# A fused four-layer graph network: the first layer's degree and weights' products behind the next block's first quarter, and two dense blocks in place of three in the third layer

## The reference

```
for each of the four layers:
    h = max(layernorm(x), 0)
    x = x + layer(h, adj)

layer 1: (adj @ h + beta * h) / (rowsum(adj) + beta) @ kernel + bias
layer 2: softmax over neighbours of adj * (h @ H_v), times h
layer 3: max([h, adj @ h] @ W.T + b, 0)
layer 4: 4-head attention over neighbours (mask adj != 0), q, k, v from h,
         out gated with x_r = h @ Ws + bs by sigmoid([out, x_r, out - x_r] @ Wb)
```

## Time and profile before

| | |
|---|---|
| median of three runs | 1193.59 us (1185.4, 1193.59, 1194.25) |
| the profiled execution's own time | 1189.68 us |
| its span | 1188.0 us |
| mean granted TensorE clock over the span | 0.85 of full speed |
| TensorE busy | 895.1 us, 75% of the span |
| VectorE busy | 822.4 us, 69% |
| ScalarE busy | 687.1 us, 58% |
| GpSimd busy | 509.9 us, 43% |
| HBM traffic | 162 GB/s over the span |

### The profile page before, as it was taken

One profiled execution on the slowest core, in us unless ns is written; L12 is line 12 of the kernel. 1 busy time (PEld: TensorE's weight loads), 2 busy tenths in 40 slices (PEclk: granted clock), 3 DMA queues, 4 the chain that ended last, 5 costly groups with the idle time before them and its releaser, 6 DMA issues.

```text
span 1188.0 us, 25534 instructions
## 1 busy us (share of the span) xinstructions
PE 895.1 (75%) x5768; PEld 569.3 (48%) x5768; DVE 822.4 (69%) x2230; ACT 687.1 (58%) x3070; POOL 509.9 (43%) x526
## 2 busy tenths in 40 slices
PE   4979999999999352666667469997667788888750
PEld 1535555556455221555556334554444555555540
DVE  7388879879788774666665761121655888888788
ACT  4999879987977031434433351000455778888762
POOL 4002767735333434555555401666214444444420
PEclk9999988988989575676665679998897999999985
DMA  9556657657450125444444538984233444444421
GB/s 367 192 207 244 241 205 290 231 203 262 170 188 27 54 86 169 133 134 134 127 121 119 179 109 343 356 290 116 89 126 111 121 116 119 120 123 122 119 72 71
DMA packets 109354, 196.19 MB, mean 165 GB/s; under 512 B 21152, under 2 KB 93088, under 8 KB 103488
## 3 DMA queue, kind: packets, MB, share of 16 engines
q1 hardware_dynamic: 84368, 74.10, 19.8%
q10 hardware_dynamic: 8448, 82.99, 18.0%
q0 software_dynamic: 16432, 37.97, 11.7%
HBM read 166.17 MB, written 25.97 MB: 162 GB/s over the span
## 4 chain that ended last, share of the span: by engine, by line
PE 42%; DVE 22%; issue 17%; ACT 7%; another core or an unknown queue 2%; DVEq 2%; SPq 1%; DMA 1%; POOL 1%; ACTq 0%; POOLq 0%
PE ps L1877 7%; PE ps L1768 7%; PE ps L1852 4%; ACT unread L936 4%; PE ps L1931 4%; DVE work L1265 4%; PE ps L1922 3%; DVE work L1575 3%; PE ps L1794 2%; PE ps L1836 2%; DVE work L1266 2%; PE ps L1720 2%; PE ps L1716 2%; PE ps L1845 1%
## 5 line engine op out<-in xcount | busy, mean ns | idle before, releaser
L936 ACT ACTIVATE unread<-work 128x128 bf16<-128x128 f32 x1024 | 300.7, 295 | 6.9 <-ACT unread L936 2.1
L1768 PE MATMUL ps<-work,h_wide 128*128 128x512 f32 x512 | 241.8, 629 | 17.3 <-ACT h_wide L848 17.3
L936 ACT ACTIVATION_READ_ACCUMULATOR unread<-work 128x1 f32 x1024 | 191.6, 187 | 0.0
L755 POOL DMA_INDIRECT work<-in_adj_rows,adj_stage x120 | 157.3, 1311 | 60.1 <-issue 32.9
L1768 PEld LDWEIGHTS ps<-work,h_wide 128*128 128x128 f32 x512 | 101.3, 203 | 140.3 <-issue 138.6
L797 POOL DMA_INDIRECT work<-h_table,stage x105 | 100.2, 954 | 126.7 <-DMA h_table<-h_wide 59.3
L797 POOL DMA_INDIRECT work<-kv_table,node_flat x93 | 89.1, 958 | 121.7 <-PE ps L1941 77.5
L1575 DVE CUSTOM_DVE_ANT_0 work<-ps,work 128x512 f32<-128x512 f32 x168 | 116.2, 747 | 22.0 <-PE ps L1922 20.0
L1931 PE MATMUL ps<-ident,work 128*128 128x128 f32 x648 | 95.9, 281 | 42.6 <-issue 22.6
L1029 ACT ACTIVATE work<-work 128x512 f32<-128x512 f32 x165 | 117.2, 713 | 11.9 <-DVE work L1584 7.8
L797 POOL DMA_INDIRECT work<-h_table,node_flat x93 | 88.5, 951 | 71.8 <-issue 38.6
(11 more groups left out here) (230 smaller groups left out, 1655.7 us busy)
## 6 DMA issues: line engine op xcount, KB each, us to landing
work<-in_adj_rows ACTq DMA_DIRECT2D x38, 2048.0 KB
work<-adj_table SPq DMA_DIRECT2D x66, 192.0 KB
work<-in_adj_rows SPq DMA_DIRECT2D x6, 2048.0 KB
mask_table<-work SPq DMA_DIRECT2D x43, 128.0 KB
work<-mask_table SPq DMA_DIRECT2D x43, 128.0 KB
work<-kv_table SPq DMA_DIRECT2D x43, 128.0 KB
adj_table<-work SPq DMA_DIRECT2D x42, 128.0 KB
work<-in_adj_rows SPq DMA_DIRECT2D x66, 64.0 KB
```

Of the source, the lines that this page charges most:

```text
L755: nc.gpsimd.indirect_dma_start(out=ag[:, h, c, :], out_offset=None, in_=adj_rows, in_offset=bass.IndirectOffsetOnAxis(ap=adj_stage[:, h // ...
L936: ins = nc.scalar.activation(unread[:, m % (MQ // 2) * TB + t, :], ring[:, q, m, t * P:(t + 1) * P], ACT.Abs, accum_out=seen[:, b, t, q * ...
L1768: ins = mm(ps[:, 0, :], h_sb[:, q * MQ + m, :], ring[:, q, m, :], start=(q + m == 0), stop=False)
```

## The change

**First layer.** TensorE's degree and weights' products of block nb, up to now at the end of that block's instructions, are a function `products(nb)`, which is called one block later: after the next block's first quarter and the positions. The positions, which stood ahead of the first quarter in the loop, stand behind it. At the end, behind the last block, they follow `places(NB - 1)`. On VectorE the copy of the block's sums to `aggT` stands between the last quarter's `half_sum` and `quarter_sum`; `place(last)` stands ahead of the first quarter's `degp`, which waits for the degree products of the block before; and `code(last, 1)` stands ahead of the second quarter's sum.

**Third layer.** DB is 2 and EACH 2, and FIXED becomes 5 by its formula: two blocks are dense, 24 tiles sparse, and a quad is followed by two dense products. ScalarE waits for all stored rows before it issues the dense loads from the third slot on, six of them in place of ten. All blocks are turned and added inside the series of quads, at two places (`quad_of_unit(T * nb + T - 1) + 2`). The list of indices is the same one; its sparse part begins four tiles earlier.

```
--- before.py
+++ after.py
@@ -56,12 +56,12 @@
 FLAT = QUADS + TURN + NBUF
 OWN_ROW = NB * P * T * TB
 ZERO_ROW = OWN_ROW + T * P
-DB = 3
+DB = 2
 DT = DB * TB
 FIXED = (T - DT) // NBUF2 - 1
 PLAIN = T // NBUF - 1
 EARLY = 4 * MQ
-EACH = (DB * T - EARLY) // (FIXED * NBUF2)
+EACH = 2
 MOST2 = (T - DT) * NP // NBUF2
 FT = 8
 GROUPS = T // FT
@@ -992,6 +992,8 @@
 
 
             act.wait_ge(slot_full[1], 16 * (NB + 1))
+            for b in range(TB):
+                act.wait_ge(row_stored[b], rows_of_before(3))
             settle(act)
             for s in range(2, DB * NQ):
                 nb, q = s // NQ, s % NQ
@@ -1001,8 +1003,8 @@
                 act.dma_start(ring2[:, q, :, :], adj_block(nb, q)).then_inc(slot_full[q], 16)
                 if nb and q == NQ - 1:
                     dense_out(nb - 1)
+            dense_out(DB - 1)
             deviations(3, slice(LAST_GROUPS[0], LAST_GROUPS[1]))
-            dense_out(DB - 1)
 
             normalise(3)
 
@@ -1258,13 +1260,18 @@
 
                 return count, tiles, firsts
 
-            def reduce_slot(nb, q):
+            def reduce_slot(nb, q, last=None):
 
                 dve.wait_ge(slot_full[q], 16 * nb + 16 if not isinstance(nb, int) else 16 * (nb + 1))
                 link = Link(dve, link_sum, 2, nb * NQ + q)
                 link(nc.vector.tensor_tensor(half_sum, ring[:, q, 0:MQ // 2, :], ring[:, q, MQ // 2:MQ, :], ALU.add))
+                if q == NQ - 1:
+                    dve.wait_ge(agg_done, nb + 1)
+                    nc.vector.tensor_copy(aggT[:, :], ps[:, 0, :]).then_inc(agg_out, 1)
                 link(nc.vector.tensor_tensor(quarter_sum, half_sum[:, 0:MQ // 4, :], half_sum[:, MQ // 4:MQ // 2, :], ALU.add))
                 link.end()
+                if last is not None:
+                    place(last)
                 if q == 0:
                     dve.wait_ge(deg_done, nb + 1)
                 nc.vector.tensor_tensor(degp[:, q, :], quarter_sum[:, 0, :], quarter_sum[:, 1, :],
@@ -1293,9 +1300,8 @@
 
             def block0(nb, last, before):
 
-                reduce_slot(nb, 0)
+                reduce_slot(nb, 0, last)
                 if last is not None:
-                    place(last)
                     code(last, 0)
                 if before is not None:
                     list_quarters(before, 3)
@@ -1304,9 +1310,10 @@
                     update(last)
                 if before is not None:
                     lists(before, 3)
+                if last is not None:
+                    code(last, 1)
                 reduce_slot(nb, 1)
                 if last is not None:
-                    code(last, 1)
                     list_quarters(last, 0)
                 reduce_slot(nb, 2)
                 if last is not None:
@@ -1314,8 +1321,6 @@
                     code(last, 2)
                     list_quarters(last, 1)
                 reduce_slot(nb, 3)
-                dve.wait_ge(agg_done, nb + 1)
-                nc.vector.tensor_copy(aggT[:, :], ps[:, 0, :]).then_inc(agg_out, 1)
                 if last is not None:
                     lists(last, 1)
                     code(last, 3)
@@ -1511,7 +1516,7 @@
                                         ALU.add).then_inc(dense_read, 1)
 
             def dense_added(j):
-                for nb in range(DB - 1):
+                for nb in range(DB):
                     if j == quad_of_unit(T * nb + T - 1) + 2:
                         add_block(nb)
                         dve.wait_ge(dense_read, nb + 1)
@@ -1532,8 +1537,7 @@
                     ins = nc.vector.bn_stats(stats[:, t, :], x_sb[:, t, :])
                 return ins
 
-            sparse_quads(dve, step2, dense_added, lambda: add_block(DB - 1))
-            dve.wait_ge(dense_read, DB)
+            sparse_quads(dve, step2, dense_added)
             products = node_terms(3)
             half = FT // 2
             rest2(2, slice(FT, 2 * FT))
@@ -1753,10 +1757,24 @@
                 pe.wait_ge(list_out, nb * TB + j + 1)
                 mm(ps[:, 7 if j % 2 else 3, P:P + NC], quarters[:, j % 2, :], sel[:, :], start=True, stop=True).then_inc(fold_done, 1)
 
+            def products(nb, first=False):
+                for q in range(NQ):
+                    pe.wait_ge(slot_summed[q], nb + 1)
+                for j in range(TB):
+                    for q in range(NQ):
+                        ins = mm(ps[:, 6, j:j + 1], degp[:, q, j * P:(j + 1) * P], ones[:, 0:1],
+                                 start=(q == 0), stop=(q == NQ - 1))
+                ins.then_inc(deg_done, 1)
+                if first:
+                    pe.wait_ge(ld, 16 * NLD)
+                pe.wait_ge(up_used, 1 + nb)
+                pe.wait_ge(agg_out, nb + 2)
+                for j in range(TB):
+                    ins = mm(ps[:, 1, j * P:(j + 1) * P], aggT[:, j * P:(j + 1) * P], k0_sb[:, :], start=True, stop=True)
+                ins.then_inc(up_done, 1)
+
             def block0(nb, last, before):
                 pe.wait_ge(agg_out, 1 + nb)
-                if last is not None and before is not None:
-                    places(last)
                 for q in range(NQ):
                     pe.wait_ge(slot_full[q], 16 * (nb + 1))
                     for m in range(MQ):
@@ -1774,8 +1792,9 @@
                         for j in range(TB):
                             ins = mm(ps[:, 0, j * P:(j + 1) * P], hbeta[:, j, :], ident[:, :], start=False, stop=(j == TB - 1))
                         ins.then_inc(agg_done, 1)
-                    if q == 0 and last is not None and before is None:
+                    if q == 0 and last is not None:
                         places(last)
+                        products(last, before is None)
                     if q == 0 and before is not None:
                         fold(before, 2)
                         a_list(before, 3)
@@ -1787,20 +1806,6 @@
                         a_list(last, q - 1)
                         if q == 2:
                             fold(last, 0)
-                for q in range(NQ):
-                    pe.wait_ge(slot_summed[q], nb + 1)
-                for j in range(TB):
-                    for q in range(NQ):
-                        ins = mm(ps[:, 6, j:j + 1], degp[:, q, j * P:(j + 1) * P], ones[:, 0:1],
-                                 start=(q == 0), stop=(q == NQ - 1))
-                ins.then_inc(deg_done, 1)
-                if last is None:
-                    pe.wait_ge(ld, 16 * NLD)
-                pe.wait_ge(up_used, 1 + nb)
-                pe.wait_ge(agg_out, nb + 2)
-                for j in range(TB):
-                    ins = mm(ps[:, 1, j * P:(j + 1) * P], aggT[:, j * P:(j + 1) * P], k0_sb[:, :], start=True, stop=True)
-                ins.then_inc(up_done, 1)
 
             block0(0, None, None)
             block0(1, 0, None)
@@ -1817,6 +1822,7 @@
             a_list(NB - 2, 3)
             fold(NB - 2, 3)
             places(NB - 1)
+            products(NB - 1)
             for j in range(TB):
                 a_list(NB - 1, j)
                 if j:
@@ -1888,15 +1894,15 @@
                 ins.then_inc(dense_turned, 1)
 
             def dense_part(j):
-                for nb in range(DB - 1):
+                for nb in range(DB):
                     if j == quad_of_unit(T * nb + T - 1) + 2:
                         turn_block(nb)
-                for n in range(EACH):
-                    dense(EARLY + EACH * j + n)
+                for u in range(EARLY + EACH * j, min(DB * T, EARLY + EACH * j + EACH)):
+                    dense(u)
 
             for u in range(EARLY):
                 dense(u)
-            last = sparse_quads(pe, neighbours, dense_part, lambda: turn_block(DB - 1))
+            last = sparse_quads(pe, neighbours, dense_part)
             pe.wait_ge(pv_read[2], NBUF2 * last + 2)
             project(3)
             pe.wait_ge(post_done[3], T)
```

71 lines of the change are left out of this document (38 added, 33 removed).

## The result

The changed kernel took **1212.6 us** (four runs, 1208.1 to 1219.0) beside 1193.6 us before (1185.4 to 1194.3): the ratio is 1.018, with an interval of 1.011 to 1.025. The change made the kernel slower by 19 us, outside the forecast range of 1172 to 1201 and clear of no change. The profiled execution took 1210.05 us, its span is 1208.2.

The account below looks back on a forecast made before the run. It took TensorE to bound the first layer and GpSimd's gathers with their pauses the third. A 12.5 us gain and an 8.1 us loss took 1189.7 to 1185.3, or 1189 us on the median; range 1172 to 1201.

Parts of the forecast that it names:

- The first layer: First layer's blocks: moving the products and the copy shortens a block from 47.15 to 45.4 us; 12.5 us gained overall.
- the half clock: TensorE's slow stretch after the degree products in each first-layer block: stays in part, 2.0 us lost per block, bounds 1.0 and 3.1.
- the third rival: First layer: the stop only moves, positions wait for flags, blocks stay near 46.8 us; 5 us gained, 1197 us; chance 0.15.
- VectorE's wait behind the last block: First layer's end: VectorE's 4.09 us wait for a list behind the weights' products goes, 1.5 us more gained.
- the prediction's first point: First layer, block's end: TensorE's 1.07 us wait for the quarter sum goes, since the copy comes about 2 us earlier.
- The wait for the stored rows: Third layer's start: with loads held back, stored rows land at 722.5; the later loads are covered by the first 16 products.
- Pauses: GpSimd's stops between third-layer gather bursts: one per four quads, five in all, 11.5 us; bounds none and eight.
- the end: Third layer's close, behind the last gathers and pauses: 1.0 us in the sum that gave 847.3 against 839.2.
- second rival: Third-layer gathers: bursts of two quads, eleven pauses, stage 22 us longer; 1203, or 1196 with milder pauses; chance 0.13.
- The first rival: Third layer: no pauses, GpSimd runs at 3.75 us a quad, 3.4 us gained there instead of 8 lost; 1177; chance 0.27.
- The range's upper end: Whole kernel: 1201 us, from eight third-layer pauses, a first-layer gain of 6.5 us, and one more us.

Follow-up runs that it names:

- experiment 7: First layer's part alone, but with the copy to aggT left in its old place behind the quarter's sum: 1135.5 us, four runs between 1121.7 and 1144.0.
- experiment 6: Changed kernel with ScalarE's dense loads held back also behind the first three quads' own rows and adjacency pieces: 1133.5 us, 7.2 less than the changed kernel.
- experiment 3: Changed kernel without ScalarE's wait for the stored rows: 1130.9 us beside 1133.5 for the kernel before, ratio 0.996.
- experiment 4: First layer's part with three dense blocks as before, plus only ScalarE's wait for the stored rows: 1136.9 us, 3.4 over the kernel before.
- experiment 9: The kernel before, unchanged, run once for its trace on another chip: 1132.6 us.
- experiment 11: The whole change run again on another chip: 1140.3 us beside 1131.9 for the kernel before, ratio 1.007.
- experiment 1: First layer's part alone, third layer as in the kernel before: 1119.1 us (four runs) beside 1133.5, ratio 0.988.
- experiment 10: First layer's part alone, run again with more rounds: 1124.8 us beside 1131.9 for the kernel before, ratio 0.993.
- experiment 12: Changed kernel with the second and third gather of each third-layer quad replaced by a plain load of 128 rows: 1118.4 us, 21.9 less than the changed kernel.

## Why the prediction was wrong

**The first layer held.** Forecast 12.5 us (6.5 to 19), a block of 45.4: measured 14.3 us and 44.5 on the first chip, 8 to 11 us in the traces on the others (448.0 against 437.1 to 439.6). The forecast had the half clock costing 2 us a block; it cost less, since the degree and weights' products took 3.68 and 1.14 us in four of the eight blocks, with a granted clock of 1.00 in the one shown, and the second quarter behind them lost only 0.8 us there (7.96 for 7.13). In no block of the loop did the positions wait for the flags, so the third rival fell. VectorE's wait behind the last block, which the prediction had go, stayed: 3.36 us of the 4.09. Experiment 7 shows that the part needs the copy's move, which is the prediction's first point.

**The step that failed is "The wait for the stored rows".** It had the loads' effect on the stores right: the gathers were released 3.5 us after the first dense product, where it had 3.1 (722.5 less 719.39). But it went on: "Queued behind ScalarE's wait are only those loads", and took the rest of the stage's first part as covered. It looked at who waits behind ScalarE and not at what the moved loads would now run beside. SyncE's own rows, three pieces of 64 KB, wait for the stored rows too. They were issued 7.6 us after the first dense product, where before they were issued 17.4 after, and came right behind three of the loads. ScalarE's loads and SyncE's own rows, after and then before:

```profile
711.82 4.89 ACTq L1003 DMA_DIRECT2D work<-in_adj_rows  x3
716.77 3.59 SPq L600 DMA_DIRECT2D work<-h_table  x3
```

```profile
726.61 7.21 ACTq L1001 DMA_DIRECT2D work<-in_adj_rows  x2
736.76 2.56 SPq L600 DMA_DIRECT2D work<-h_table  x3
```

After, 6 MB had been issued in the 5 us ahead of the own rows; before, the last two loads had been issued 10.2 and 3.3 us ahead of them. So it is not enough that loads run beside: they did before, and the own rows were there within 10.2 us. The view of DMA queues, after, from 720 to 744 (queue: packets, MB, share):

```profile
q10 hardware_dynamic: 600, 8.78, 88.4%
q0 software_dynamic: 324, 0.64, 7.5%
q1 hardware_dynamic: 600, 0.45, 5.7%
```

ScalarE's queue (q10) and SyncE's (q1) were served 600 packets each in 24 us. But a packet of ScalarE's is 14.6 KB (8.78 MB over 600) and one of SyncE's 0.75, so SyncE's queue moved 0.45 MB in 24 us. With the loads held back it moved 0.81 MB in 8 (experiment 6). Before, from 722 to 736:

```profile
q10 hardware_dynamic: 353, 5.00, 84.2%
q1 hardware_dynamic: 977, 0.71, 15.2%
```

SyncE's queue got 977 packets in 14 us beside ScalarE's 353, and the own rows issued at 736.76 were there at 746.97, when TensorE began the first quad. That ScalarE's queue, with its loads 7 us apart, did not hold work all the time then fits this, but no view shows it. The Trainium skill, DMA: Bandwidth & Descriptors (section Queues, rings and completion order), says that each DMA engine goes round the queues that it has work for, packet by packet; the equal counts of 600 agree, if the profile's packets are the page's. Experiments 3, 4 and 6 show the cause of the late own rows: without ScalarE's wait the stop goes, with the wait and three blocks it is there, and with the loads behind the own rows these land in 1.9 us. On the first chip it made the fifth quad's gathers start 40.3 us after the first dense product (749.46) where the prediction had 29.1 (748.5 less 719.39): **11.2 us of the error**.

**"Pauses" was mis-sized, and rests on the chip.** Forecast were five pauses of 2.3 us, 11.5 in all; the trace after has six, the first after two quads and the others after each four as forecast, of 2.2 to 6.6 us. They sum to 21.3, or 19.5 beyond the 0.3 that lies between any two gathers. The fifth quad's first gather to VectorE's turn to the fourth layer took 108.8 us for 98.8 forecast: **10 us of the error**, 8 of them the pauses and 2 the end (3.5 us from the last gather's end to VectorE's turn, for 1.0). With the 11.2 that is the third layer's whole miss (29.3 for 8.1). The longest pause (6.59) is 3.4 us over the ones beside it, by VectorE's work at the second block's end, which the prediction had no term for. Experiments 9 and 11 show the signals in time on another chip, and there the change costs 12.7 us in the stage (119.6 for 106.9) where it costs 33.4 on the first (145.8 for 112.4). So 20.7 us of the stage's loss there go with the late signals. They hold up a later quad's own rows as well, since SyncE waits for the same signal before it loads them (TensorE waits 9.19 us for one at 852.68). No run shows what part that is, nor why the signals are late. The prediction named this as its second rival, with two quads a burst; it was four, with longer pauses.

**The first rival's premise came true elsewhere, and its number not.** Without late signals GpSimd runs at 3.75 us a quad, but the stage is 12.7 us longer, not 3.4 shorter: 7.3 for the wait (119.6 against 112.3 without it) and 5.4 for the exchange of 32 dense products for four quads (112.3 against 106.9). The rival let the wait bring forward the fifth quad's gathers; it delays them, by 7.4 us (40.2 for 32.8), which is the 7.3. And the exchange changes the engine that sets the stage. Before, it is TensorE's 32 dense products and 16 steps of 4.33 us; after, without the wait, GpSimd's gathers without a pause: 17.8 us to the first, 24 quads at 3.75 are 90.0, and 4.5 more to the last addition make the 112.3. A rough sum, not tested by itself: TensorE's step falls from 4.33 to 2.61 us, but GpSimd's 3.75 comes next, so only 0.58 us of each of 16 steps can be had, 9.3, against four quads at 3.75, 15.0. That is 5.7 lost, near the 5.4 measured.

**Two of its sums are off.** The range's upper end, from its own terms (the stage 3.4 shorter without pauses, eight pauses 18.4, first layer 6.5, and one more), is 1203 and not 1201. The 1196 of the second rival goes with the middle gain of the first layer, 12.5; with the low one it is 1202. The time measured lies beyond all of these.

The version to keep is that of experiments 1 and 10, the first layer's part alone: 0.993 of the kernel before, and better than the whole change by 15.5 us on the same chip. It was not measured on the first chip.

## What to carry to other kernels

When a big load is moved to a later time, list every small transfer of every queue that is issued in the time that it moves into, with its packets, and ask what waits for each; a small load of small packets that is issued right behind big ones of another queue can take as long as they do (29.8 us here), and one that comes when they are further apart can be through in 10. Work moved from one engine to another is worth no more than the distance to the engine that is next, here 0.58 us a step and not 1.72, and costs its full price there; when it stops being the slowest engine, look for what sets the stage now. And a forecast of 4 us for two opposite effects of 12 and 8 is one where each part should be made to stand by itself.

## What the runs showed of the hardware

The same kernel took 1193.6 us in the first set and 1132 to 1133 in the three others. In the third layer of the first set's two traces VectorE saw TensorE's products up to 10.8 us late while GpSimd issued gathers without a pause, and 2.0 to 2.5 us after it stopped; GpSimd itself went on at about the same time (776.65 beside 776.04). In the others' third layer VectorE saw them 0.2 us after their end where it waited for them, with the same program before and the same gathers (GpSimd's 1.25 us apiece in both). The granted clock is no plain reason: before, in the first layer it was 0.92 in the slow trace and 0.93 in the fast one, in the third 0.97 and 1.00. In the second layer it was 0.63 and 0.77, and that layer took 37 us more in the slow case; whether late signals, the clock, or both made that longer is not shown. Why the signals are late is open: no later run showed them, so nothing could be tried against it, and experiment 12's part on the pauses stays unanswered.
